# Routing inside the cross attention's loop, and work moved from VectorE to ScalarE and TensorE, in a two-layer decoder

## The reference, cut to what matters

```python
x = x + self_attention(layernorm(x))                    # 16 heads of 16, bias
q = layernorm(x) @ Wq.T + bq; k = ctx @ Wk.T + bk; v = ctx @ Wv.T + bv
s = clip(q k^T / 4, -50, 50); s = where(mask, s, -50)
p = softmax(s); p = p / (p.sum() + 1e-8)
d = clip(rs, 0, 0.3) * ((p v) @ Wo.T + bo)
x = x + layernorm(d) * gamma + beta
h = rmsnorm(layernorm(x)) * norm_w                      # mixture of experts
w, ids = top_k(softmax(h @ gate_w.T), 4); w = w / w.sum()
# each expert takes its first 256 tokens in order: buf[expert, position] = h
out = silu(buf @ Wg) * (buf @ Wu) @ Wd                  # per expert, 32 of them
x = x + layernorm(x) + sum_k w_k out[slot_k] + shared_expert(h)
```

## Time and profile before

| what | value |
|---|---|
| three runs | 1044.99, 1045.81, 1052.66 us; median 1045.81 |
| the profiled execution | 1049.7 us, of which the profile's span is 1047.9 |
| mean granted clock of TensorE | 0.912 of 2.4 GHz |
| busy over the span | PE 829.2 us (79%), DVE 673.1 (64%), ACT 486.8 (46%), POOL 321.5 (31%) |
| DMA | 90.71 MB, mean 87 GB/s |

### The profile page before, as it was taken

The page is one execution under the profiler, slowest core; times in us unless marked ns, Lnnn a source line. Parts: engine busy times, 40 slices in busy tenths (PEclk is TensorE's granted clock), DMA queues, the critical chain, the costliest instruction groups (busy, mean ns, idle before and its releaser), DMA issues. The chain is left out here.

```text
span 1047.9 us, 16118 instructions
## 1 busy us (share of the span) xinstructions
PE 829.2 (79%) x5470; PEld 545.3 (52%) x5470; DVE 673.1 (64%) x1381; ACT 486.8 (46%) x1235; POOL 321.5 (31%) x281
## 2 busy tenths in 40 slices
PE   3899762347997078767888988897649999999997
PEld 2677642216875066623666766666524444444443
DVE  3778964635764279557788777883346565656654
ACT  1765431115566046514565555654244544454453
POOL 1113763660000554324445424440021221211210
PEclk9999975578999599869999999999659999999999
DMA  9900003227985211000000000000115443444431
GB/s 311 419 29 2 2 2 131 72 80 221 329 301 180 60 48 55 1 1 1 1 1 1 0 0 1 1 1 1 48 50 142 122 123 105 130 115 113 132 91 41
DMA packets 35398, 90.71 MB, mean 87 GB/s; under 512 B 6406, under 2 KB 8969, under 8 KB 34826
## 3 DMA queue, kind: packets, MB, share of 16 engines
q1 hardware_dynamic: 32266, 81.63, 24.4%
q0 software_dynamic: 3072, 8.30, 2.5%
HBM read 67.71 MB, written 22.29 MB: 86 GB/s over the span
## 5 line engine op out<-in xcount | busy, mean ns | idle before, releaser
L1199 POOL TENSOR_TENSOR m1ws<-m1raw,m1ws 128x768 f16<-128x768 f32 x33 | 55.0, 1669 | 219.0 <-ACT m1raw L1202 219.0
L733 POOL TENSOR_TENSOR xqr<-xqr,xt 128x512 f32<-128x512 f32 x48 | 61.2, 1276 | 140.7 <-DVE xt L1069 140.7
L1509 DVE TENSOR_TENSOR m1sg<-m1sg,m1Wb 128x512 f32<-128x512 f32 x66 | 61.1, 926 | 64.0 <-ACT m1sg L1427 53.1
L1469 PE MATMUL m1pg<-m1hs,m1ws 128*128 128x512 f16 x396 | 97.5, 383 | 3.8 <-PEq L58 3.8
L1480 PE MATMUL m1py<-m1ap,m1ws 128*128 128x512 f16 x396 | 96.3, 379 | 1.6 <-DVE m1ap L1521 1.6
L1469 PE MATMUL m1pu<-m1hs,m1ws 128*128 128x512 f16 x396 | 97.0, 381 | 0.0
L1431 ACT ACTIVATE m1ap<-m1ac 128x512 f16<-128x512 f32 x66 | 41.6, 630 | 116.1 <-DVE m1ac L1515 116.1
L1521 DVE TENSOR_TENSOR m1ap<-m1ac,m1ap 128x512 f16<-128x512 f32 x66 | 45.7, 693 | 45.9 <-ACT m1ap L1431 45.9
L1565 POOL DMA_INDIRECT rows<-slots_out,slot x32 | 32.7, 1022 | 116.5 <-DMA slots_out<-m0yo 103.4
L1469 PEld LDWEIGHTS m1pg<-m1hs,m1ws 128*128 128x128 f16 x396 | 38.9, 98 | 51.3 <-issue 5.3
L1480 PEld LDWEIGHTS m1py<-m1ap,m1ws 128*128 128x128 f16 x396 | 38.6, 98 | 48.8 <-DVE m1ap L1521 2.6
(11 more groups left out here) (289 smaller groups left out, 1921.5 us busy)
## 6 DMA issues: line engine op xcount, KB each, us to landing
m1Wb<-wt_dram SPq DMA_DIRECT2D x66, 256.0 KB, 4.0
m1raw<-in_m_w SPq DMA_DIRECT2D x33, 384.0 KB, 4.2
slots_in<-zeros SPq DMA_DIRECT2D x1, 8192.0 KB, 26.6
m0rg<-in_m_wgu SPq DMA_DIRECT2D x16, 512.0 KB, 6.9
m0xg<-slots_in SPq DMA_DIRECT2D x32, 256.0 KB, 4.6
slots_out<-m0yo SPq DMA_DIRECT2D x32, 256.0 KB, 3.6
m0rd<-in_m_wd SPq DMA_DIRECT2D x8, 512.0 KB, 7.6
xwo<-in_x_wo SPq DMA_DIRECT2D x1, 2048.0 KB, 17.8
```

Source lines behind the costliest of these rows:

```text
L733: pool.tensor_tensor(blk, blk, t2[:, k % 2, :, :], ALU.add).then_inc(add_ok, 1)
L1199: pool.tensor_tensor(ws[:, u, 1, :], raw[:, u, :], ws[:, u, 0, :], ALU.subtract).then_inc(prep_ok, 1)
L1469: ins = pe.matmul(bank[:, :], part(ws, u, sw, c, which), hs[:, sh, c, CH * q:CH * q + CH], start=(k == 0), stop=(k == 5))
L1509: dve.tensor_tensor(sg[:, q, :], sg[:, q, :], Wb[:, u, CH * q:CH * q + CH], ALU.mult).then_inc(sw_ok, 1)
```

## The change

- **Routing tile by tile.** A class `Routing` holds the routing's steps for one tile. `attention16` issues them in its cross iterations: stats(i-2) on VectorE, its root on GpSimd, norm(i-2) and rows(i-2) on ScalarE, turn(i-2) on TensorE, then logits(i-3), choose(i-3), places(i-4), place(i-4), and on GpSimd the scatters two at a time. What is left after n = 15 has an order of its own. Seven tiles are scattered in this block (`LATE` = 7), the last in the experts' block. The routing's own block is gone. x takes its second term by eight ScalarE activations (`update`).
- **ScalarE copies context first.** A crossed exps(n) reads the scores from PSUM; VectorE clips the exponentials in SBUF afterwards (`clip`). k_mask and v_copy of crossed tiles are ScalarE activations (eight of 128x128, four of 64x128), behind ct_copy and before pt_copy and h_out in its queue.
- **The V bias** is a third matmul with one row of ones.
- **The delta's norm.** droot's four GpSimd operations become one more step in residual (times gamma) and one scalar_tensor_tensor (`finish`), both on VectorE.
- **The split** of the second layer's weights moves into the experts' loop: high at k = 1, 4, ... 22 on ScalarE (one copy instead of two), low at k = 2, 5, ... 23 on VectorE.
- **Loads.** The routing's and the first experts' loads are issued in `ahead`. Large tiles of a0 lie in the room of later tables (`Room`).

```diff
             def exps(n):
                 u = n % 2
+                if crossed(n):
+                    act.wait_ge(s_ok, n + 1)
+                    act.activation(sc[:, u, :, :].rearrange("p (r h) k -> p r (h k)", r=2), p_s[:, :, :], ACT.Exp, scale=QSCALE).then_inc(exp_ok, 1)
+                    return
...
+            def k_mask(n):
+
+                act.wait_ge(qk_ok, n + 1)
+                for g in range(DC):
+                    for i in range(QH):
+                        ins = act.activation(KB[:, g, i, :], p_kg[:, g, :], ACT.Identity, scale=hmask[:, i:i + 1], bias=bm[:, g, i:i + 1])
+                ins.then_inc(k_out, 1)
...
+            def clip(n):
+                u, i = n % 2, n - CROSS
+                dve.wait_ge(exp_ok, n + 1)
...
+                for b in range(2):
+                    half = E[:, :, :, S * b:S * b + S]
+                    ins = dve.tensor_scalar(half, half, EXP_LOW, hiE[:, 2 * i + b:2 * i + b + 1], ALU.max, ALU.min)
+                ins.then_inc(clip_ok, 1)
...
+                    dve.scalar_tensor_tensor(d, d, dmv[:, u, 0:1], of(n, "gamma")[:, :], ALU.subtract, ALU.mult).then_inc(l_step, 1)
...
+            def finish(n):
...
+                dve.scalar_tensor_tensor(x[:, i, :], dl[:, u, :], dmv[:, u, 3:4], x[:, i, :], ALU.mult, ALU.add).then_inc(fin_ok, 1)
+                dve.wait_ge(fin_ok, i + 1)
```

More of the change, by code:

```diff
@@ L191, in droot, with scatter @@
                 pool.tensor_tensor(dmv[:, u, 3:4], dmv[:, u, 2:3], neghalf[:, 0:1], ALU.pow).then_inc(drstd_ok, 1)
[L192 to L199, removed]
+            def scatter(n, *ks):
+                if 0 <= n < LATE:
+                    pool.wait_ge(route.slot_ok, n + 1)
+                    for k in ks:
+                        route.slots.scatter(pool, n, k)
             if slots:
@@ L273, in _ @@
                     ct_copy(n - 1)
-                if not crossed(n):
+                routed(lambda e, j: route.logits_out(e, j), i - 3, act)
+                if n + 1 < TILES and crossed(n + 1):
+                    if n + 1 == CROSS:
+                        act.wait_ge(ready, 1)
+                    k_mask(n + 1)
+                    v_copy(n + 1)
+                routed(lambda e, j: route.norm(e, j), i - 2, act)
+                routed(lambda e, j: route.rows(e, j), i - 2, act)
+                if n < CROSS:
                     pt_copy(n)
@@ L277, in _ @@
                     h_out(n + 2)
-                if crossed(n):
-                    split.high(act, n - CROSS)
+                routed(lambda e, j: route.exps(e, j), i - 3, act)
+                if route and n == NT - 2:
+                    route.slots.shared_high(act)
             ct_copy(TILES - 1)
+            if route:
+                route.logits_out(act, NT - 3)
+                route.norm(act, NT - 2)
+                route.rows(act, NT - 2)
+                route.logits_out(act, NT - 2)
+                route.norm(act, NT - 1)
+                route.rows(act, NT - 1)
+                route.exps(act, NT - 3)
+                route.logits_out(act, NT - 1)
+                route.exps(act, NT - 2)
+                route.exps(act, NT - 1)
+                route.update(act)
         @block.tensor
@@ L2129, in decoder @@
         w_c0["count"] += 16
-        with first.stack:
-            attention16(nc, C, "a0", (("self", w_a0), ("cross", w_c0)), ahead=ahead, split=split)
-        rows = SlotRows(g, C, RopeTables(g, a, split.raw))
-        C["rope"] = rows.rope
-        moe_slots(nc, C, a, rows)
+        with mo.stack:
+            with first.stack:
+                attention16(nc, C, "a0", (("self", w_a0), ("cross", w_c0)), ahead=ahead, route=lambda m: Routing(m, C, a, bufs),
+                            room=Room(*(t.rearrange("p a b -> p (a b)") for t in (rope.red.rearrange("p a b c -> p a (b c)"),
+                                        rows.rows.rearrange("p a b c -> p a (b c)"), rope.ang[:, :, :], rope.turns[:, :, :]))))
+            moe_slots(nc, C, a, rows, bufs, split)
         attention16(nc, C, "a1", (("causal", w_a1),), slots=rows)
```

1040 lines of the change are left out of this document (554 added, 486 removed).

## The result

Four runs of each: 1019.54 us after (1016.31 to 1020.56), 1047.18 before (1044.99 to 1052.66); ratio 0.972, 95% interval 0.968 to 0.977. The forecast was 1018, from a term sum of -27.7; the medians differ by 27.6. The agreement is better than its terms are, as the stretches show.

What follows compares the result with a forecast made beforehand. VectorE's queue was taken to pace the cross attention, a chain of hand-offs the routing, TensorE the experts. Terms +15.5, +2, -34.4, -11.8, -1, +2 sum to -27.7; off 1045.8 that gives 1018 us, range 1004 to 1036.

Steps and rivals of the forecast that it cites:

- Part 1: Cross-attention loop, n = 8 to 15: with VectorE's new steps the iterations take 79 us against 63.4, +15.5.
- rival of a chain between the engines: Cross loop from n = 10 and tail: engines wait for each other in queue order, +15, 1033 us; chance 0.17.
- sign of being wrong: Cross loop on VectorE: the forecast is wrong if each clip takes 0.42 us; it had priced 0.68 each.
- rival of the two-port mode: Cross loop on VectorE: the clip runs two columns a cycle, -2.5 us, 1015 or 1016; chance 0.1.
- Part 2: Cross loop's other engines: ScalarE 7.1 us, TensorE 8.6, GpSimd 8.3 a tile; k_mask's eight activations 2.3 (2.1 to 2.5).
- Part 3: Hand-over from self to cross attention, n = 7: pt_copy(7) waits behind k_mask(8) and v_copy(8), +2 (0 to +3.5).
- Part 4: Tail from o_norm(15) to the expert block: 62.4 us become 28, with GpSimd's scatter(6) ending last, -34.4.
- Part 5: Expert block's start to first transposes: four scatters left, TensorE's shared expert ends last, -11.8; better clock, -1.
- Part 6: Expert loop: the weight split's ScalarE copies and VectorE instructions cost +2 (0 to +13).
- Bound by DMA: Experts: DMA sets the loop, so its end follows the first load, -15.5 us, 1015; chance 0.15.
- Slow indirect DMAs: GpSimd's scatters blocked by VectorE: tail 24 us more, n = 13 to 15 +13, 1055; chance 0.04.
- Full price of the split: Expert loop grows by the weight split's whole price, +11, 1029 us; chance 0.1.

Runs made afterwards that it cites:

- experiments 2: Changed kernel with TensorE's places moved from the head of the iteration to behind qk and turn_ctx: 1013.8 us, ratio 0.970.
- experiment 5: Changed kernel with LATE = 4, so sixteen scatters are left to the experts' block: 1026.7 us, ratio 0.982.
- Experiment 1: Changed kernel with the clip's lower bound taken from a one-column tile instead of an immediate: 1016.6 us, ratio 0.972.
- experiment 9: Changed kernel without the weight split in the expert loop, the last attention working on zeros: 1018.2 us.
- experiment 8: Kernel before with only the weight split moved from the cross loop into the expert loop: 1040.9 us against 1045.5, ratio 0.996.
- experiment 6: Changed kernel with pt_copy(7) ahead of k_mask(8) and v_copy(8) on ScalarE, pv(7) ahead of scores(8) on TensorE: 1019.5 us.
- experiment 7: Changed kernel with the K mask of all crossed tiles back on VectorE instead of ScalarE: 1014.0 us, ratio 0.970.
- experiment 4: Changed kernel with LATE = 6, so eight scatters are left to the experts' block: 1016.2 us, ratio 0.971.
- the second profile of before: Kernel before, unchanged, profiled once more for its expert loop: 93.5 us there against 96.3 in the first profile.

## Why the prediction was right, and where it was not

- **Part 1, VectorE's iterations (+15.5, measured +17.7).** 1.8 of the 2.2 too little is in n = 8 (10.1 us, 8.3 forecast). At full clock 8.3 is what it takes: experiments 2 and 5 show 8.34, with some luck, since k_mask took 0.6 more than its term and the other steps of the chain as much less. In the changed kernel TensorE idled ahead of it and its clock fell to 0.76; the forecast had no clock term there. For n = 11 to 15 it had 9.5, 11.2, 11.9, 10.8 and 9.9; measured 9.2, 11.0, 12.9 (12.1 at full clock), 10.9 and 9.5. The sizes are right and the reason half wrong: the claim "VectorE leads by 2 us" from n = 12 failed, for VectorE waits 1.1 us for project at n = 12, 1.5 at n = 14 and, at full clock, 0.5 at n = 13 (2.1 with the slow clock), which is the forecast's rival of a chain between the engines, weaker than it was priced. The clip, 0.5 us cheaper per tile than its 1.36, hid a part of that in the sum.
- **The clip.** The step that failed is "the row shows 0.413, so I side with the row". A row with one width gives no pace: 0.413 was split into too small a fixed part and too large a slope. The prediction's other row, L624 with 1536 columns in 0.959 us, is 0.62 ns a column all told and spoke against one column a cycle already. Experiment 1 has the same form at two widths, and the slope is 0.5 ns a column. The rule that was turned down (the Trainium skill, VectorE: DVE Perf Modes, Mode 2×_2P: two columns a cycle for fp32 from SBUF to SBUF) holds for both L423 and the clip; what the 0.28 us worked out by it lacked is the fixed part of two tile scalars. So the forecast's own sign of being wrong, a clip of 0.42 us, is what the profile shows (0.43 to 0.48), and its rival of the two-port mode had the mechanism. That rival gave -2.5 us; experiment 1 shows for 0.12 us per tile that the time hangs on the clip only at n = 15. What 0.5 us more would have cost no run shows.
- **Part 2, the other engines.** k_mask took 2.9 to 3.04 us for its eight, above the upper end of 2.5: activations with a scale and a bias from tiles start 0.35 to 0.37 us apart, not 0.27. It is in the chain of n = 7 and 8. GpSimd's root(15) behind two scatters was seen rightly as a wait, 0.8 forecast and 0.71 measured at full clock (experiment 9). The stall behind the weight split went (L593 at 0.17 us); experiment 8 prices the split's move at -4.7 us of the cross loop.
- **Part 3, the hand-over (+2, measured +2.1).** Right size in part by luck: at full clock it is +1.3 (9.2 to 9.3 us in experiments 2 and 5), the rest is the clock. What has to go for the two iterations to get shorter is k_mask ahead of scores(8), not k_mask ahead of pt_copy(7): experiment 6 moved the copy and gained nothing in the sum of the two, and experiment 7 took k_mask out of the chain and gained 2.2 there and 1.1 in n = 8 against the full-clock profiles.
- **Part 4, the tail (-34.4, measured -33.6).** Right to the engine and the instruction that ends it. VectorE ended at 22.9 (21.8 forecast), and GpSimd at 24.7 (25). The gap behind it was 4.1 us, not 3.0; the cause is open, since the kernel before ends the stage on an indirect DMA too.
- **Part 5, the start of the experts (-11.8, measured -12.1, and -1 for the clock, measured -1.5).** With four scatters left TensorE's shared expert ends last, as forecast; with eight (experiment 4) the loads do, by 1.5 us, and with sixteen (experiment 5) by 11.8. The warm start was some 0.5 more than its term.
- **Part 6, the split in the experts (+2).** Measured 0.2 in experiment 9, less than executions differ by; experiment 8, with the split added to the kernel before, has no longer loop either. The late stores did not turn it into a delay.
- **Rivals.** Bound by DMA: no, the loop takes 88.9 to 92.3 us in all changed kernels, wherever it starts, and does not get shorter when it starts 8 us later (91.7 in experiment 5). Slow indirect DMAs: no, beside VectorE's short instructions they kept 0.97 to 1.2 us. Full price of the split: no.

The close hit thus is in part luck. It holds two errors that cancel: some 2.8 us too little up to the experts, no more than the slow clock of this execution cost in the hand-over, n = 8 and n = 13 (0.8, 1.7 and 0.8), and some 4 too much in them (-3.1 against the second profile of before, forecast +1), with some 2 us of noise in either median.

## To carry to other kernels

Where work is shared out anew among engines, ask in each stretch which wait ends last: the K mask is better on VectorE in the two tiles in which ScalarE's chain feeds TensorE; in the later ones VectorE has more to do and the runs do not tell the two places apart (72.7 us on ScalarE and 74.1 on VectorE for n = 9 to 15, each with clock dips of its own). A step that waits for the end of another engine's iteration does not belong at the head of an in-order queue; here it cost 0.3 to 0.5 us an iteration. Before a wait is blamed on the order of the work, read the granted clock of its stretch: of the 2.10 us at n = 13 only 0.47 were left at full clock. And a duration at one width is no rate; take two widths of one form before pricing a third.

## What the runs showed of the hardware

- A fp32 tensor_scalar from SBUF to SBUF: 412 ns for 256 and 541 for 512 columns with two tile scalars, 481 for 512 with one tile scalar and one immediate.
- TensorE's granted clock (means over an iteration, between the levels of 1.2 and 2.4 GHz) turns small waits into large ones. With the same code, iteration 8 took 8.3 us at full clock (experiments 2 and 5) and 10.1 at 0.76 (changed kernel, experiment 4), and iteration 13 12.1 at full clock (experiment 9) and 12.9 at 0.87 (changed kernel). In iteration 7 TensorE had idled 2.0 us in all of these profiles, whether the clock then fell or held, so that the idle time alone does not tell which iteration is hit, and a removed wait of a microsecond can show as nothing.
- From the last instruction of a block to the first matmul of the next: 2.6 us where VectorE's work was last (experiments 4 and 5), behind an indirect DMA 4.1 in the changed kernel and 3.0 in the kernel before.
